# Attention over pairs of heads: masks moved from TensorE to VectorE and GpSimd, the value products regrouped, and one product that adds and turns the outputs

## The reference, cut to what matters

```python
q = (x @ Wqa @ Wqb).reshape(b, s, H, D)              # b=2, s=2048, H=16, D=16
kv = (x @ Wkva @ Wkvb).reshape(b, s, KVH, D, 2)      # KVH=4
q, k, v = _rope(q), _rope(kv[..., 0]), kv[..., 1]
k, v = repeat(k, 4, axis=2), repeat(v, 4, axis=2)
scores = einsum('bqhd,bkhd->bhqk', q, k) * D ** -0.5
scores = where(triu(ones((s, s)), k=1), -inf, scores)
out = einsum('bhqk,bkhd->bqhd', softmax(scores), v).reshape(b, s, E)
return out @ Wout + bout
```

## Time and profile before

| | |
|---|---|
| executions | 2581.57, 2591.58, 2600.53 us |
| median | 2591.58 us |
| profiled execution, first to last instruction (the profile gives this execution no other time) | 2609.7 us |
| attention, first A piece (214.5 us) to the last product | 1083.5 us |
| instructions in the profiled execution | 44812 |
| TensorE / VectorE / ScalarE / GpSimd busy | 86% / 68% / 45% / 30% of the span |

### The profile page before, as it was taken

One profiled execution on the slowest core, in us unless ns is written; L12 is line 12 of the kernel. 1 busy time (PEld: TensorE's weight loads), 2 busy tenths in 40 slices (PEclk: granted clock), 3 DMA queues, 4 the chain that ended last, 5 costly groups with the idle time before them and its releaser, 6 DMA issues. The chain is left out here.

```text
span 2609.7 us, 44812 instructions
## 1 busy us (share of the span) xinstructions
PE 2234.0 (86%) x12898; PEld 1283.6 (49%) x12898; DVE 1772.8 (68%) x3458; ACT 1179.7 (45%) x2552; POOL 772.4 (30%) x613
## 2 busy tenths in 40 slices
PE   5866889999999999999879999967578887798777
PEld 2322333333333333333369999946345544454446
DVE  3656667778887778777433333346498889988892
ACT  1222556666666666666644454411123333343332
POOL 3333333000000000000023333355156666566651
PEclk9756989999999999999989999976689898898897
DMA  7423333111111111111142223156400000000004
GB/s 280 130 70 104 96 104 103 57 56 58 58 58 56 58 56 58 57 57 57 30 146 94 97 81 109 49 159 196 145 1 16 17 17 0 16 16 16 9 0 141
DMA packets 140179, 191.32 MB, mean 73 GB/s; under 512 B 19256, under 2 KB 116416, under 8 KB 137920
## 3 DMA queue, kind: packets, MB, share of 16 engines
q1 hardware_dynamic: 111392, 139.92, 16.6%
q0 software_dynamic: 9120, 31.47, 3.7%
q10 hardware_dynamic: 19584, 18.88, 2.1%
HBM read 125.34 MB, written 60.29 MB: 71 GB/s over the span
## 5 line engine op out<-in xcount | busy, mean ns | idle before, releaser
L912 DVE TENSOR_REDUCE at_piece_max<-at_A 128x1 f32<-128x512 f32 (+3 forms) x1280 | 740.9, 605 | 249.3 <-PE at_A L809 205.9
L778 ACT ACTIVATE at_wt<-at_B 128x512 f32<-128x512 f32 (+3 forms) x1280 | 607.9, 537 | 339.1 <-PE at_B L833 211.9
L806 PE MATMUL at_A<-at_ka,at_qa 96*128 96x512 bf16 (+3 forms) x1280 | 459.1, 361 | 79.2 <-DMA at_ka<-k_parts 76.2
L830 PE MATMUL at_B<-at_qb,at_kb 99*128 99x512 bf16 (+3 forms) x1280 | 446.2, 353 | 1.7 <-ACT at_wt L778 0.6
L850 PE MATMUL at_O<-at_wt,at_v 128*32 128x512 f32 (+3 forms) x2496 | 339.2, 548 | 0.4 <-ACT at_wt L778 0.4
L806 PEld LDWEIGHTS at_A<-at_ka,at_qa 96*128 96x128 bf16 x1280 | 126.2, 99 | 432.7 <-DVE at_piece_max L912 245.8
L1176 POOL TENSOR_TENSOR s_down<-lw_down_full,s_down 128x256 fp32r<-128x256 f32 x10 | 7.3, 729 | 873.9 <-ACT lw_down_full L1168 873.9
L1353 PE MATMUL ex_H<-ex_xT,ex_w_in 128*128 128x256 f32 x1920 | 247.5, 285 | 3.2 <-DVE ex_xT L1460 3.2
L1353 PEld LDWEIGHTS ex_H<-ex_xT,ex_w_in 128*128 128x128 f32 x1920 | 236.6, 192 | 3.6 <-DVE ex_w_out L1465 3.6
L2051 POOL TENSOR_TENSOR l_sumy<-l_sumy,l_scaled 128x1024 f32<-128x1024 f32 x72 | 220.1, 3057 | 27.9 <-ACT l_scaled L2201 26.6
L2251 DVE TENSOR_TENSOR l_order<-l_order 128x1024 f32<-128x1024 f32 x112 | 221.2, 1975 | 1.9
(11 more groups left out here) (246 smaller groups left out, 3191.2 us busy)
## 6 DMA issues: line engine op xcount, KB each, us to landing
buf<-zeros POOLq DMA_DIRECT2D x10, 1024.0 KB, 20.6
ex_x<-buf SPq DMA_DIRECT2D x40, 256.0 KB, 2.7
expert_out<-ex_y ACTq DMA_DIRECT2D x40, 256.0 KB, 2.2
at_v<-v SPq DMA_DIRECT2D x32, 256.0 KB
ex_raw_in<-in_W_in SPq DMA_DIRECT2D x8, 1024.0 KB, 4.9
q_parts<-parts SPq DMA_DIRECT2D x16, 384.0 KB, 4.5
at_qa<-q_parts SPq DMA_DIRECT2D x32, 192.0 KB
at_ka<-k_parts SPq DMA_DIRECT2D x32, 192.0 KB
```

Of the source, the lines that this page charges most:

```text
L778: act.activation(wt[p % NE_][:, q0:CH], pB_of(p, u)[:, q0:CH], ACT.Exp, scale=D ** -0.5).then_inc(wt_ready, 1)
L806: ins = pe.matmul(pA[b][:, 0:w], qa[u][:, i * P:(i + 1) * P], ka[u][:, k0:k0 + w], start=True, stop=not diag)
L830: ins = pe.matmul(pB_of(p, u)[:, q0:CH], kb[u][:, kt * P:(kt + 1) * P], qb[u][:, j * CH + q0:(j + 1) * CH], start=True, stop=not diag)
L912: dve.tensor_reduce(piece_max[:, i, k0 // CH:k0 // CH + 1], pA[a_step(p) % NA][:, 0:w], AX.X, ALU.max).then_inc(a_used, 1)
```

## The change

Rounds are over pairs of heads (`HP = 2`), 16 of them. The two heads of a pair share the k stack and the values, so one pair's loads are nine DMAs for A and ten for B. On TensorE, A and B pieces of the two heads alternate: A(h0) B(h0) A(h1) B(h1) at each p. The buffers for A and for B in PSUM stay three each. `wt` grows from 8 to 20 tiles.

- Neither kind of piece gets its mask from TensorE any more. On a diagonal A piece VectorE adds a mask tile `hide` and takes the maximum with one `tensor_tensor_reduce`, whose elementwise output goes to one of four `junk` tiles. On a B piece nothing is added; after the exponential GpSimd sets the hidden part of its 128x128 diagonal block in `wt` to zero (`affine_select`), and `values` waits for it (`hidden`).
- `values` is over four key tiles of both heads, eight products (16 instructions, since an f32 product is two). The row group is 2h + kt mod 2, so a column group gets two products in turn. The widened first product is gone; two small products with a zero tile `blank` clear the rows that kt = 1 doesn't reach.
- `turn` multiplies the copied bank with a 128x64 matrix `summing` of zeros and ones instead of the identity, which adds the two row groups of each head and turns in one. ScalarE copies the sums and their denominators to `s["attn"]`, now 128 x 32 x 16 x 17 (`keep`); the three VectorE instructions of `result` are gone.
- The division moves to `mixing`: VectorE takes the reciprocals of all sums at its start, and GpSimd multiplies step by step (at the end of its step, after the indirect DMAs) into `at`, which SyncE no longer loads. GpSimd's first step waits for the reciprocals.
- GpSimd's copies to the expert slots are spread over the 16 rounds, two tiles each, between the selects.
- The counterpart of a semaphore, the places of the maxima's turns (after p = 6 and p = 18) and of the copies follow; `LAG` stays 3.

```diff
-        NA, NB, NE_ = 3, 3, 8
+        NA, NB, NE_ = 3, 3, 20
...
             def piece_a(n, u, p, h):
...
-                ins = pe.matmul(pA[b][:, 0:w], qa[u][:, i * P:(i + 1) * P], ka[u][:, k0:k0 + w],
-                                start=True, stop=not diag)
-                if diag:
-                    ins = pe.matmul(pA[b][:, w - P:w], identb[:], hide[:, 0], start=False, stop=True)
+                pe.matmul(pA[slot % NA][:, 0:w], qa[u][:, h, i * P:(i + 1) * P], ka[u][:, k0:k0 + w],
+                          start=True, stop=True).then_inc(a_made, 1)
...
             def values(n, u, p4):
-                pe.wait_ge(wt_ready, NPC * n + p4 + 4)
+                pe.wait_ge(wt_ready, PER_B * n + HP * (p4 + VG))
+                wait(pe, hidden, PER_D * n + DIAG[p4 + VG])
...
+                    for h in range(HP):
+                        rows = slice(VW * (2 * h + kt % 2), VW * (2 * h + kt % 2 + 1))
...
             def turn(n, j):
-                    ins = pe.transpose(pX_of(j)[:, t, :], raw[j % 2][:, t * P:(t + 1) * P], ident[:])
+                    ins = pe.matmul(pX_of(j)[:, t, :], raw[j % 2][:, t * P:(t + 1) * P], summing[:], start=True, stop=True)
...
             def maximum(n, p, h):
+                if diagonal:
+                    ins = dve.tensor_tensor_reduce(junk[(HP * i + h) % 4][:, 0:w], pA[slot % NA][:, 0:w], hide[:, CH - w:CH], 1.0, NEG,
+                                                   ALU.add, ALU.max, accum_out=top)
+                else:
+                    ins = dve.tensor_reduce(top, pA[slot % NA][:, 0:w], AX.X, ALU.max)
...
+            def causal(n, p, h):
+                j, kt, q0 = Bp[p]
+                N = PER_B * n + HP * p + h
+                block_ = wt[(HP * p + h) % NE_][:, q0:q0 + P]
+                pool.wait_ge(wt_ready, N + 1)
+                pool.affine_select(block_, block_, [[1, P]], ALU.is_ge, 0.0, base=0,
+                                   channel_multiplier=-1).then_inc(hidden, 1)
...
-                sp.dma_start(at[u][:], s["attn"][:, bass.ds(2 * t, 2), :]).then_inc(x_in[u], 16)
...
+                pool.tensor_tensor(at[u][:].rearrange("p w (h n) -> p w h n", n=D), s["attn"][:, both, :, 0:D],
+                                   over_sum[:, both].unsqueeze(3).to_broadcast([P, 2, H, D]),
+                                   ALU.mult).then_inc(at_ready, 1)
...
+            dve.reciprocal(over_sum[:], s["attn"][:, :, :, D]).then_inc(sums_inverse, 1)
```

More of the change, by code:

```diff
@@ L787, in _ @@
+                    for jj in range(NQ):
+                        late = jj == NQ - 1
+                        if late and first:
+                            continue
+                        if p == (END[jj] + LAG) % NPC:
+                            raw_copy(n - late, jj)
+                        if p == (END[jj] + LAG + VG + 1) % NPC:
+                            keep(n - late, jj)
             for n in range(2):
                 round_(n, n, n == 0)
-            with act.Fori(1, HEADS // 2) as j:
+            with act.Fori(1, HPAIRS // 2) as j:
@@ L902, in _ @@
+            values(HPAIRS - 1, 1, NPC - VG)
+            turn(HPAIRS - 1, NQ - 1)
         @block.vector
         def _(dve):
[L904 to L913 removed]
+            dve.memset(blank[:], 0.0).then_inc(filled, 1)
@@ L959, in _, with round_ @@
-            CUT_1 = {0: (0,), 1: (1, 2), 2: (3, 4)}
-            CUT_0 = {HALF[0] + k: (k,) for k in range(5)}
-            def round_(n, first, ahead):
+            CUT_1 = {k: k for k in range(CUTS)}
+            CUT_0 = {HALF + k: k for k in range(CUTS)}
+            def round_(n, ahead):
                 for p in range(NPC):
                     if ahead:
-                        maximum(n + 1, p)
-                    for step in CUT_1.get(p, ()):
-                        cut_max(n, 1, step)
+                        for h in range(HP):
+                            maximum(n + 1, p, h)
+                    if p in CUT_1:
+                        cut_max(n, 1, CUT_1[p])
@@ L977, in round_ @@
-                    for j in range(NQ):
-                        step = (p - END[j] - LAG - 3) % NPC
-                        if step < 3:
-                            if j < NQ - 1:
-                                result(n, j, step)
-                            elif not first:
-                                result(n - 1, j, step)
+                    if ahead and p in CUT_0:
+                        cut_max(n + 1, 0, CUT_0[p])
+                    if ahead and p == M0_AT:
+                        max_copy(n + 1, 0, PER_A * (n + 1) + M0_SLOT, M0_SLOT % NA)
@@ L985, in _ @@
             for p in range(NPC):
-                maximum(0, p)
+                for h in range(HP):
+                    maximum(0, p, h)
                 if p == M1_AT:
-                    dve.wait_ge(a_used, M1_AT + 1)
-                    dve.sem_inc(a_used, 1)
-                for step in CUT_0.get(p, ()):
-                    cut_max(0, 0, step)
+                    dve.wait_ge(a_used, M1_SLOT)
+                    dve.sem_inc(a_used, 2)
+                if p in CUT_0:
+                    cut_max(0, 0, CUT_0[p])
@@ L992, in _ @@
                 if p == M0_AT:
[L993 to L1002 removed]
+                    max_copy(0, 0, M0_SLOT, M0_SLOT % NA)
@@ L1005, in layer1_weights @@
+            for n in range(HPAIRS):
+                round_(n, n + 1 < HPAIRS)
 def layer1_weights(nc, d, s):
```

421 lines of the change are left out of this document (208 added, 213 removed).

## The result

Median 2628.51 us (four executions, 2621.12 to 2630.95) against 2591.89 us for the kernel before: ratio 1.0135, interval 1.0102 to 1.0168 (95%; the plain quotient of the two medians is 1.0141). The change makes the kernel slower by 1.35%; the forecast was 2550 us. The profiled execution has a span of 2628.8 us, 19.1 more than the one before.

A forecast was written before the change was run, and what follows sets the result against it. Attention was taken as bound by TensorE plus waits, afterwards by VectorE freeing three banks for eight pieces. Attention -53.7 us (1083.5 to 1029.8) and mixing +12 made -42 from 2591.6: 2550 us, range 2485 to 2640.

The forecast's parts named there:

- A round at full clock: Attention, per pair of heads: 57.8 us of stretches plus 3.6 for masked maxima, 61.4 us, where two rounds took 66.5.
- a masked maximum: VectorE, diagonal A pieces: 0.15 us above a plain maximum, ends 0.07 and 0.31; each 0.1 adds 2.4 us per round.
- my formula: Attention round: ten stretches, 57.8 us, plus the masked extra for 24 of the 32 masked maxima.
- My ten stretches: Attention round, between values after p = 2, 6, ..., 38: 6.5, 6.1, 5.5, 7.0, 5.6, 5.5, 6.1, 5.4, 5.6, 4.4, together 57.8 us.
- half rate: Rival, VectorE: masked maxima take two cycles per column, 8.5 us more per round, 2688 us; chance 0.12 with other dear maxima.
- The slot copies, on GpSimd and the same DMA engines, are spread out.: Attention rounds: waits for loads taken as gone despite the copies; loads staying late would give back 15 x 1.5 us.
- the upper of its two levels nearly throughout: Attention rounds of the kernel before: granted clock 0.97, the upper level being 2.4 GHz.
- the waits for loads as gone: Attention rounds: loads have 61 us for 1.4 times the bytes of a 33 us round, so no waits.
- Prelude and last round: Attention ends: 80 maxima ahead of round 0, 47.3 us and 0.5 to start; last round and its copies 56 us.
- Mixing: Stage mixing: GpSimd starts some 8 us later, then 0.4 to 1 us over 16 steps; together +12 us, ends 0 and 25.
- late selects: Rival, GpSimd in attention: from 1.2 us per select, each 0.1 adds 3.2 us per round; 2700 us at 1.5; chance 0.06.
- TensorE stays the bound: Rival, attention: banks free sooner than 0.73 us, rounds near 52 to 54 us, 2430 us; chance 0.10.

## Why the prediction was wrong

The forecast was 42 us less, measured are 37 more. The span of the profile was to be 2568 us and is 2628.8. Of these 61 us some 53 lie in the attention, 6 in mixing and 2 between the two. By its steps:

- **A round at full clock: right in sum, partly by luck.** 61.4 us were forecast. Without gap and seam it is 60.1. Two terms were off against each other: a masked maximum costs 0.01 us more than a plain one, not 0.15, which makes 58 us by my formula, and the formula left out ScalarE. Its three banks hold TensorE up as well, now that eight pieces B come in one stretch, by 2.6 us per round as worked out above. TensorE's own terms came out: a full group of values takes 1.85 us to the next start and 0.1 more ahead of it, a diagonal one 1.42, a turn 0.94. The waits for banks behind VectorE, "in sum some 8 us per round", are 6.3. (My ten stretches add up to 57.7, not 57.8, and half rate to 8.1 us per round, not 8.5; neither matters.)
- **The step that failed** is the sentence "The slot copies, on GpSimd and the same DMA engines, are spread out." I put them at nothing because they were spread over rounds, and didn't ask how close together they stand within one. They stand four in a row, once per round, and cost 1.2 to 1.7 us each time and the clock behind it: 3.7 us per round on average (65.1 with them, 61.4 without), 56 us in fifteen rounds, as much as the attention missed its forecast by. Moved to pairs, the kernel is at 0.9917, 2570 us on the scale of the forecast.
- **The rounds before.** I took 66.5 us for two of them, a mean over two kinds. The six rounds in which most of the copies are made take 34.8 to 37.9 us, with the clock at 0.91 to 0.95 and waits of 2.3 to 4.9 us for the k stack. The other 25 take 32.3 on average. Against two of those the 60.1 us of a round without gap and seam are a gain of 4.5 us, not of 6.4. So the rounds with the copies were the dear ones in the kernel before too, though the copies come in pairs there; whether the price is theirs or that of other transfers beside them was not tried. Rows of single rounds would have shown it.
- **The clock.** I took it from the earlier trace rows as given, "the upper of its two levels nearly throughout", and wrote its fall down only as a sign of error. But gaps that had hardly any consequence in the kernel before (0.97 there, with waits of 0.5 to 2.1 us for `at_ka` in its steady rounds) had one here, where TensorE also waits for banks in every stretch. That this is the reason is my reading. In rounds without a seam gap and clock cost 4.6 us (64.7 against 60.1), of which the gap is about 1.7 (61.8 at full clock).
- **The seam.** I took the waits for loads as gone, rightly, but didn't say what is late next. It was the jump, 2.4 us every second round, which cost nothing visible in the kernel before and comes with packets of instructions in this one, and its share of low clock: rounds with it take 3.7 us more. The Trainium skill ("Runtime: NRT & Kernel Launch", section "Instruction fetch mechanics") says that a taken branch out of the fetched window stalls the engine until its target has been fetched. The gaps of 2.1 to 2.6 us on TensorE and 2.4 on ScalarE, gone when written out, and the packets of instructions around them agree with this.
- **Prelude and last round:** 47.8 and 56 us were forecast; the prelude took 44.4, and what lies outside it and the fifteen measured rounds 62.3, partly at lower clock.
- **Mixing:** the mechanism and the start were right (8 us forecast, 8.0 measured), the product in GpSimd's chain costs 0.69 us at every step, inside the 0.4 to 1 that I wrote, but next to nothing of it was hidden or given back by the loads: 18 instead of 12. Another 2.2 us lie between the attention and the experts, whose first load is issued later; they were not looked into.
- **The scale.** The profiled execution of the kernel before was 18 us above the median, and I carried that difference over. That of the changed kernel is not above its median, so 18 us of the 78 by which 2550 was missed are this step alone.
- **The rivals:** none came true. Half rate and late selects are refuted by the 689 and 292 ns rows. The rule of the Trainium skill cited there is about two sources in SBUF; for one source in PSUM, one in SBUF and a bf16 result the trace shows no halving. "TensorE stays the bound" came nearly true only when the stretches were cut to two positions.

The time itself, 2628.5, lay in the range; the sign was wrong, and the case that made it so was in none of my rivals.

## What to carry to other kernels

A burst of indirect DMAs is not free because it is on an idle engine: look how closely they follow each other, and issue them in twos. When a change makes the body of a loop longer, look for packets of instructions at its jumps. Read length and clock of single rounds, not the mean of a stage: gaps of 1.5 us cost three times their length when the clock follows, and a mean can hide rounds of two kinds. A stage in which one engine feeds two others through three banks each should change between kinds of work often, not in long runs.

## What the runs showed of the hardware

- With four indirect DMAs of 128 rows issued 1.3 us apart, TensorE's signals for finished products are held up and come together, six within 0.17 us, 5.7 to 6.4 us after the first of the four. VectorE and ScalarE start 1.5 to 2.0 us late for it, both at the same time. With two and two and 6.3 us or more between them this doesn't happen. Why transfers should hold up signals is open.
- The clock doesn't fall after every gap: with gaps of 1.1 to 1.9 us and TensorE otherwise busy it held in 11 of 13 rounds; with gaps of 1.2 to 1.6 us, groups of four positions and no loops, in seven of 11.
- The jump of a loop cost TensorE 2.1 to 2.6 us in the kernel that fetches instructions throughout (108 packets in 800 us), and nothing that can be seen in the one that fetches none in that stretch; code written out is fetched too (73 packets) and shows no gap over 1 us at a seam.
- A masked maximum through PSUM with a bf16 by-product takes 689 ns for 512 columns, 6 more than the plain one, and the 128x1 instruction behind it (0.08 us) is hidden.
- GpSimd's select over 128x128 takes 292 ns, VectorE's reciprocal of 128x512 numbers 3.35 us.
